# A decoder layer in one launch: V in 512-column products, the T2 products regrouped, an arc tangent series by products, and every engine's calls in a new order

## The reference

```python
x = _layernorm(x + attn(x))        # 16 heads of 16; logits against 64 latent keys, top 4 of them,
                                   # softmax over the 4, their weighted sum plus V, times Wo
x = _layernorm(x + xattn(x, ctx))  # 16 heads; scores against 64 context rows with rotary angles,
                                   # softmax over the 64, context, w_kc_kv, times Wo
x = _layernorm(x + ffn(x))         # three ternary linear layers; silu(a) * b between them

def _ternary_quant(w):
    s = jnp.mean(jnp.abs(w))
    wq = jnp.round(jnp.tanh(w / (s + EPS))) * jnp.arctanh(s)
```

## Time and profile before

| what | value |
|---|---|
| median of three runs | 349.58 us (349.52 to 349.66) |
| the profiled execution | 349.29 us |
| its span, first to last instruction | 347.6 us |
| PE busy | 330.5 us, 95% of the span, 2539 instructions |
| DVE busy | 287.0 us, 83% |
| ACT busy | 281.4 us, 81% |
| POOL busy | 251.9 us, 72% |
| granted clock of PE | 0.999 of full speed |
| transfers | 17.58 MB, nearly all before 43 us |

### The profile page before, as it was taken

One profiled execution on the slowest core, in us unless ns is written; L12 is line 12 of the kernel. 1 busy time (PEld: TensorE's weight loads), 2 busy tenths in 40 slices (PEclk: granted clock), 3 DMA queues, 4 the chain that ended last, 5 costly groups with the idle time before them and its releaser, 6 DMA issues.

```text
span 347.6 us, 7479 instructions
## 1 busy us (share of the span) xinstructions
PE 330.5 (95%) x2539; PEld 243.4 (70%) x2539; DVE 287.0 (83%) x718; ACT 281.4 (81%) x535; POOL 251.9 (72%) x228
## 2 busy tenths in 40 slices
PE   8999999999789899999999999999999999999893
PEld 4767776787567676787777767777778777666341
DVE  2667296999599999898789999999889877998882
ACT  2857899886479399888988898988987988999783
POOL 3357536999889698898658888779749757577561
PEclk9999999999999999999999999999999999999999
DMA  7999700000000000000000000000000000000001
GB/s 224 414 412 417 270 0 2 0 4 2 0 0 3 1 2 0 17 0 4 15 2 17 16 3 1 17 0 18 2 0 18 15 3 15 15 2 16 18 16 45
DMA packets 5653, 17.58 MB, mean 51 GB/s; under 512 B 624, under 2 KB 3056, under 8 KB 4720
## 3 DMA queue, kind: packets, MB, share of 16 engines
q1 hardware_dynamic: 5616, 17.12, 12.9%
HBM read 15.02 MB, written 2.10 MB: 49 GB/s over the span
## 4 chain that ended last, share of the span: by engine, by line
PE 60%; DVE 18%; POOL 10%; issue 8%; ACT 3%; POOLq 0%; DVEq 0%; ACTq 0%
PE wide L524 9%; PE small L562 8%; PE wide L583 5%; PE wide L508 4%; PE wide L445 3%; PE small L432 3%; PE wide L457 3%; PE small L480 3%; PE small L606 3%; PE small L484 3%; PE wide L539 3%; PE wide L550 2%; DVE m L1073 2%; PE small L469 2%; PE wide L355 2%
## 5 line engine op out<-in xcount | busy, mean ns | idle before, releaser
L562 PE MATMUL small<-V_sb,PT_sb 128*128 128x256 f32 x256 | 58.5, 381 | 1.3 <-DVE y_row L1104 1.3
L562 PEld LDWEIGHTS small<-V_sb,PT_sb 128*128 128x128 f32 x256 | 47.7, 190 | 8.9 <-DVE y_row L1104 1.5
L1339 POOL TENSOR_TENSOR Ls<-Ls,m 128x1024 f32<-128x1024 f32 x16 | 32.3, 2019 | 29.0 <-DVE mask L1087 29.0
L524 PE MATMUL wide<-B_sb,x1T 128*128 128x512 f32 x192 | 49.6, 407 | 0.0
L1073 DVE MAX8 m<-Ls 128x8 f32<-128x64 f32 x256 | 33.9, 210 | 11.5 <-ACT Ls L774 10.4
L1402 POOL TENSOR_TENSOR region_c<-region_c,region_q 128x1024 f32<-128x1024 f32 (+1 forms) x17 | 32.3, 1902 | 13.8 <-DVE region_c L1197 11.6
L524 PEld LDWEIGHTS wide<-B_sb,x1T 128*128 128x128 f32 x192 | 35.4, 188 | 9.8 <-issue 1.2
L1354 POOL TENSOR_TENSOR Ls<-Ls,mask 128x1024 f32<-128x1024 f32 x16 | 37.8, 2365 | 1.3 <-ACT Ls L787 0.5
L1377 POOL TENSOR_TENSOR P<-P,r 128x1024 f32<-128x1024 f32 x16 | 32.6, 2036 | 6.8 <-DVE r L1141 6.8
L1346 POOL TENSOR_TENSOR mask<-mask,r 128x1024 f32<-128x1024 f32 x16 | 30.4, 1902 | 8.0 <-DVE r L1096 6.9
L583 PE MATMUL wide<-tern,region_k 128*128 128x512 bf16 x128 | 32.1, 379 | 0.7 <-ACT region_k L888 0.6
(11 more groups left out here) (184 smaller groups left out, 868.7 us busy)
## 6 DMA issues: line engine op xcount, KB each, us to landing
region_q<-in_wqx SPq DMA_DIRECT2D x1, 2048.0 KB, 16.7
region_c<-in_woTx SPq DMA_DIRECT2D x1, 2048.0 KB, 8.5
out_x<-region_q SPq DMA_DIRECT2D x16, 128.0 KB, 1.7
first<-in_xT SPq DMA_DIRECT2D x7, 256.0 KB, 9.9
region_c<-in_wkcqT SPq DMA_DIRECT2D x1, 1536.0 KB, 11.6
region_r<-in_wqkr SPq DMA_DIRECT2D x1, 1024.0 KB, 7.5
region_r<-in_w1T SPq DMA_DIRECT2D x1, 1024.0 KB, 11.0
region_t<-in_w2T SPq DMA_DIRECT2D x1, 1024.0 KB, 12.8
```

The costliest lines, as they stand in the source:

```text
L524: mm = pe.matmul(ps_L2[:, r * 512:(r + 1) * 512], x1T[:, u, k, :], B_sb[:, s, w, k, r * 512:(r + 1) * 512], start=(u == w == k == 0), stop ...
L562: mm = pe.matmul(ps_O2[:, 0:D], PT2_sb[:, c, :], V_sb[:, c, :], start=(c == 0), stop=(c == PAIRS - 1))
L1339: pool.tensor_tensor(heads(Ls[n % 2][:]), heads(Ls[n % 2][:]), over_heads(m8[:, :, 0:1]), ALU.subtract).then_inc(g_d1, 1)
```

## The change

Four things are changed.

- `V_` multiplies in 4 products of 512 columns instead of 8 of 256. It does this for two value blocks at a time, since they lie at a fixed distance in `C_sb`. The four 64 x 64 quarters of the array are each used once in every four products, before and after.
- `T2_` makes the same 32 products. They come in groups of four with the full depth of 128 rows and then four with 64 rows, where before two of the one kind and two of the other took turns.
- `atanh_series` raised the mean to eight odd powers with one power instruction over 128 x 24. Now it makes them by products: a square, then doublings of the list of terms. The input `series` loses its exponents.
- All lists of calls are new. With them some PSUM names are: `ps_T2` is `wide[2]`, `ps_T1` is `(wide[2], wide[1])`, `ps_C` is `(wide[2], wide[2])`, `ps_S3` is `small[1]`, and three others near the end.

```diff
-        ps_T2 = wide[0]
+        ps_T2 = wide[2]
-        ps_S3 = small[0]
+        ps_S3 = small[1]
-        ps_T1 = (wide[2], wide[0])
+        ps_T1 = (wide[2], wide[1])
-        ps_C = (wide[0], wide[2])
-        ps_Z_last = (wide[1], wide[0])
-        ps_HT_last = (wide[1], small[0])
+        ps_C = (wide[2], wide[2])
+        ps_Z_last = (wide[1], wide[2])
+        ps_HT_last = (wide[2], small[0])
...
-                for i in range(PAIRS):
+                for i in range(PAIRS // 2):
                     for u in range(2):
-                        for e in range(2):
-                            c = (i + e * PAIRS // 2) % PAIRS
+                        for e, c in ((0, i), (1, i + PAIRS // 2), (1, i), (0, i + PAIRS // 2)):
...
-                for c in range(2):
+                for e in range(2):
                     for r in range(2):
                         rows = slice(r * L, (r + 1) * L)
-                        for e in range(2):
-                            mm = pe.matmul(ps_V[half][e * L:(e + 1) * L,
-                                                      r * 512 + c * D:r * 512 + (c + 1) * D],
-                                           kv[rows, b, :], C_sb[rows, 2 * half + c, e, :],
-                                           start=True, stop=True)
+                        mm = pe.matmul(ps_V[half][e * L:(e + 1) * L, r * 512:(r + 1) * 512], kv[rows, b, :],
+                                       C_sb[rows, 2 * half:2 * half + 2, e, :], start=True, stop=True)
...
-                link(pool.tensor_tensor(terms[:], mean.rearrange("p (w o) -> p w o", o=1)
-                                        .to_broadcast([P, 3, TERMS]), exponents, ALU.pow))
-                link(pool.tensor_tensor(terms[:], terms[:], coefs, ALU.mult))
+                link(pool.tensor_tensor(square, mean, mean, ALU.mult))
+                link(pool.tensor_tensor(terms[:, 0], mean, square, ALU.mult))
+                for k in (1, 2, 4):
+                    link(pool.tensor_tensor(terms[:, k:2 * k], terms[:, 0:k], prep[:, 6:7, :]
+                                            .to_broadcast([P, k, 3]), ALU.mult))
+                    if k < 4:
+                        link(pool.tensor_tensor(square, square, square, ALU.mult))
...
```

```diff
-            warm(9, wide[0]); Q(0); warm(4, wide[0], p_warm, 1); L1(0); T1_(0)
+            warm(9, wide[0]); Q(0); warm(4, wide[0], p_warm, 1); L1(0); T1_(0); T1_(1, a_L1, 1)
```

More of the change, by code:

```diff
@@ new lines, in _ @@
+            exp_1(0); copy_L1(1); centre_wo(); keep_T2(); copy_PT1(0); exp_4(1); copy_T2()
+            exp_1(1); copy_L1(2); copy_A(0); copy_Q(2); copy_A(1); copy_AT(0); exp_4(2)
+            copy_B(0, 0); copy_PT1(1); exp_1(2); copy_B(1, 0); sum_abs(0); copy_L1(3)
+            sum_abs(1); copy_B(2, 0); sum_abs(2); copy_AT(1); square_1(0); copy_PT1(2)
+            norm_1(0); copy_C(0); copy_Q(3); copy_B(3, 0); exp_4(3); copy_X1(0); square_1(1)
+            copy_L1(4); exp_1(3); norm_1(1); copy_C(1); exp_4(4); copy_AT(2); copy_X1(1)
@@ new lines, in _ @@
+            copy_B(2, 1); copy_AT(6); whole_x2(0); copy_B(3, 1); copy_XQ(0); norm_1(5)
+            copy_V(1, 1); copy_X1(4); copy_PT2(2); exp_4(7); square_1(6); norm_2(1); exp_1(7)
+            copy_V(0, 1); tanh(0); square_x2(1); copy_X1(5); square_2(2); copy_PT2(3); exp_2(4)
+            norm_2(2); square_h(0); exp_4(8); copy_V(1, 2); square_x2(2); whole_x2(1)
+            whole_h(0); copy_XQ(1); exp_1(8); norm_1(6); copy_HT(0); copy_PT1(7); copy_L1(9)
+            copy_AT(7); tanh(1); copy_PT1(8); exp_2(5); square_2(3); copy_X1(6); square_3(0)
@@ new lines, in _ @@
+            copy_PT2(4); square_1(7); norm_1(7); copy_AT(8); norm_2(3); whole_x2(2)
+            copy_V(0, 2); square_x2(3); copy_XQ(2); square_h(1); exp_2(6); copy_L1(10); exp_4(9)
+            tanh(2); exp_1(9); copy_Q(6); whole_x2(3); whole_h(1); copy_PT2(5); copy_XQ(3)
+            square_1(8); copy_HT(1); copy_PT1(9); exp_4(10); square_h(2); square_3(1)
+            square_2(4); tanh(3); norm_2(4); copy_X1(7); square_x2(4); copy_AT(9); copy_V(1, 3)
+            whole_h(2); whole_x2(4); copy_B(0, 2); square_2(5); exp_1(10); norm_1(8)
@@ new lines, in _ @@
+            copy_B(1, 2); copy_L1(11); norm_2(5); copy_PT2(6); square_x2(5); copy_XQ(4)
+            copy_HT(2); copy_PT1(10); square_h(3); copy_AT(10); copy_X1(8); square_1(9)
+            exp_4(11); copy_B(2, 2); copy_V(0, 3); norm_1(9); exp_2(7); square_1(10)
+            copy_B(3, 2); square_3(2); tanh(4); copy_Q(7); copy_L1(12); exp_1(11); whole_h(3)
+            whole_x2(5); copy_PT2(7); square_2(6); copy_XQ(5); norm_2(6); copy_HT(3)
+            square_h(4); exp_4(12); exp_1(12); square_3(3); square_x2(6); norm_1(10); exp_2(8)
@@ new lines, in _ @@
+            copy_X1(9); copy_V(1, 4); copy_PT1(11); whole_h(4); tanh(5); square_2(7)
+            whole_x2(6); copy_L1(13); copy_X1(10); copy_HT(4); norm_2(7); copy_XQ(6)
+            copy_AT(11); square_h(5); copy_PT1(12); copy_V(0, 4); square_x2(7); exp_4(13)
+            copy_PT2(8); copy_AT(12); square_1(11); exp_2(9); square_3(4); tanh(6); norm_1(11)
+            copy_L1(14); whole_h(5); whole_x2(7); square_1(12); exp_1(13); copy_XQ(7)
+            square_2(8); copy_X1(11); copy_HT(5); copy_PT2(9); exp_2(10); square_h(6); tanh(7)
@@ new lines, in _ @@
+            exp_4(14); square_3(5); whole_h(6); norm_2(8); norm_1(12); copy_B(0, 3)
+            square_x2(8); exp_1(14); copy_PT1(13); copy_V(1, 5); square_2(9); copy_L1(15)
+            copy_HT(6); whole_x2(8); copy_AT(13); copy_X1(12); norm_2(9); copy_PT1(14)
+            copy_B(1, 3); exp_2(11); copy_B(2, 3); copy_AT(14); square_1(13); copy_XQ(8)
+            square_x2(9); copy_B(3, 3); copy_V(0, 5); norm_1(13); square_h(7); exp_4(15)
+            copy_PT2(10); exp_1(15); whole_h(7); square_3(6); tanh(8); whole_x2(9); square_1(14)
@@ L1294, in _ @@
             mean, one_m, ratio, ln_in, ln_out = (prep[:, k, :] for k in (1, 2, 3, 4, 5))
[L1295 removed]
+            square, acc, small = (prep[:, k, :] for k in (6, 7, 10))
             chain = [0]
```

385 lines of the change are left out of this document (173 added, 212 removed).

## The result

The changed kernel takes 356.45 us in the median of four runs (355.79 to 357.20), beside 349.55 for the kernel before. The ratio is 1.0199, with a 95% interval from 1.0186 to 1.0212: slower by 2%, where 346.0 was predicted. The profiled execution took 357.2 us.

The account below looks back on a forecast made before the run. PE bounds the kernel, busy 330.5 of 347.6 us, with a four-engine chain in the middle. 349.29 - 1.14 - 0 - 0.45 + 1.3 - 3.3 + 0 = 345.7, plus 0.29 for the median: 346.0 us, range 344.5 to 348.

Parts of the forecast that it names:

- T2: T2_ on PE: fewer changes between depth 128 and 64 take it from 5.88 to 4.74 us, 1.14 less.
- V: V_ calls on PE: 512 columns cost the same as 256; term 0, bounds 0 and 1.3 us less.
- Neighbours: PE calls up to O2(15): costs depend on the calls around them; the new list gives 0.45 us less.
- The front: New PE stalls before the middle, from the T1 copy and ACT's copies and sums: 1.3 us more.
- The middle: 40 to 140 us: less work on DVE, ACT and POOL removes most PE stalls, 3.3 of 5.62 us.
- The tail: From the start of O2(15) to the end: term 0, bounds 1.5 us either way, 33 us long.
- the stalls of the middle only move: Rival: the new order makes other stalls in the chains of the middle; 349.3 us, no change; chance 0.15.
- The slower one: Rival: the first ternary on DVE delays low_B(3, 0) and the first L2 by 5.2 us; 353.2 us; chance 0.10.
- T2 stays: Rival: T2_ on PE stays at 5.88 us, so the kernel takes 347.1 us; chance 0.10.
- all chains loosen: Rival: no PE stall in the middle and none new in front; 342.4 us; chance 0.15.
- if PE's losses in the middle were 5 us again with other names: Sign against the forecast: PE's stalls in the middle come to 5 us again, at other waits.

Follow-up runs that it names:

- series_later_old_order: The kernel before with the three new parts and its old order, POOL's series moved behind root_2(0), shift_1(6), gain_x(0), root_1(4) and roots_x(0); 349.56 us.
- ternary_1_behind_max_2: The three new parts in the old order, with ternary(1) on DVE moved some 6 us later, behind max_2(3); 349.52 us.
- the two moves on DVE: The changed kernel with gaps_4(4) to (7) directly behind top_4 and ternary(1) moved behind residual_1(4); 353.96 us.

## Why the prediction was wrong

- **T2: right in size.** 4.74 us forecast, 4.69 measured, also in the old order. The change turned the order of the column halves too, and no run separates that from the grouping by depth. The rule of the Trainium skill (TensorE: Matmul & The Clock Gate, Part 3, The mechanism), that a weight load runs under a matmul only when the row group differs, was taken to mean that regrouping gives nothing; the traces show 1.19 us less.
- **V: right**, 1.02 to 1.09 us a call as before.
- **Neighbours:** no run tests the 0.45 us alone. Open.
- **The front: near in size, by luck, and wrong in place.** 1.3 us forecast, 1.8 measured. The first `L2` started at 51.8 (51.2 forecast). `S3` and `O1(1)` didn't wait, and `B_(2, 0)` did for 0.26 us of the 0.5. `X1T(0)` waited 0.88 us for `copy_Q(3)`, which stands behind `copy_C(0)` on ACT, 3 us that my walk had left out. No run moved that copy.
- **The middle: this step failed.** It said of the stalls: "With 5 us less in the middle on each of DVE, ACT and POOL I expect most of them to go", 3.3 us less. The loss from 52 to 150 us went from 5.5 to 11.8 us instead, 6.3 more. Three things were wrong in it. First, the 4.2 us of POOL and the 5.2 of DVE were priced from rows that held waits: the earlier trace rows has 1.25 us for a multiply which takes 0.24, and the earlier trace rows 2.88 for a DVE instruction which takes 1.27 elsewhere, both beside the other engine's work. The form of the series is worth 2.4 us of POOL where DVE leaves room and 0.3 where it doesn't, and PE got 0.3 us of it at most. Second, an engine's sum of work doesn't set these stalls. In `series_later_old_order` and `ternary_1_behind_max_2` waits of 2.7 us were taken away or shortened, and 3.2 and 3.0 us stood in their place. Third, the new order brought a cost that the sum had no term for: DVE and POOL wait for each other by the instruction, so that a subtraction of 0.22 us takes up to 2.43. Of the wait of 3.17 us ahead of `PT1(5)`, 1.3 came of that, and behind it PE ran at half clock for 6.8 us, which cost 2.8.
- **Behind 150 us** the forecast had no term, and 1.6 us more were lost, in waits of 0.2 to 0.7 us each.
- **The tail: right**, 33.1 us behind the start of `O2(15)`, where 33 was forecast.

The sum as measured: 349.29 - 1.2 - 0.45 + 1.8 + 6.3 + 1.6 + 0.2 = 357.5, beside 357.2. The 0.45 in it is the forecast's own, and 0.3 us are unexplained. Of the 6.3, 2.8 are the clock in this execution, and less in the other three.

Of the rivals, "the stalls of the middle only move" came nearest to the mechanism, but held them to their old size and had neither the exclusion nor the clock. The slower one put the blame on the first `ternary`, which ran from 43.5 to 47.1 us, in time, and whose move changed nothing. "T2 stays" and "all chains loosen" fell. That I would be wrong "if PE's losses in the middle were 5 us again with other names" was the sign to look for.

What stays open: with the two moves on DVE the new order is still 5.8 us behind the new parts in the old order. The table places 6.0 us of loss (front 1.8, 52 to 100 1.0, 100 to 150 1.6, behind 1.6), but no run ties the last two to single calls. They are waits of 0.2 to 0.9 us for all of ACT, DVE and POOL. The 1.8 us of the front have a wait that the trace names, but no run of their own either. So of the 8.3 us that the new order costs, the moves on DVE gave back 2.5; the cause of the rest is open in detail.

## What to carry to other kernels

- A duration in a trace can be a wait. Before pricing an instruction on DVE or POOL, compare it with its shortest row, and look for one on the other engine that ends at the same time.
- A forecast that adds up durations by engine doesn't know of what two engines deny each other, nor of the clock. Move work only after naming the chain that it stands in; work that leaves a busy engine, but not the chain, gives nothing.
- Where a wait of some 3 us on PE can't be removed, try to fill it. In the two kernels where this was done, the clock stayed up behind it, and the runs lay within 0.5 and 1.1 us of each other (1.4 and 3.1 without).

## What the hardware showed that I had not expected

- DVE's 128 x 64 subtraction of two SBUF inputs takes 0.22 us, and 2.43 beside a POOL product; POOL's 128 x 3 product takes 0.20 us, and 1.17 beside a DVE product.
- Waits of the same length can end differently for the clock: behind 3.17 us it fell to half, behind 3.16 us in another kernel's fastest run it did not. That kernel's ten runs spread over 3.1 us, with mean clocks from 0.997 down to 0.989, and over 1.1 us once the gap was filled.
- Regrouping `T2_`'s products by depth, and with it the order of the column halves, with the same 64 instructions, took 1.19 of 5.88 us off it.
